# Reciprocal roots with a third-order last turn, and the key sum masked in one operation

## The reference

```
x = x + 0.5 * ffn(layernorm(x))
x = x + attention(layernorm(x))
x = x + 0.5 * ffn(layernorm(x))
```

```
q = elu(x @ Wq.T + bq) + 1;  k = elu(x @ Wk.T + bk) + 1;  v = x @ Wv.T + bv      # per head
kv = einsum('bthd,bthe->bhde', k, v)
denom = einsum('bthd,bhd->bth', q, k.sum(axis=1))
out = einsum('bthd,bhde->bthe', q, kv) / clip(denom, 1e-06)
return out @ Wo.T + bo
```

## Time and profile before

| | us |
|---|---|
| median of 3 runs | 501.38 |
| lowest, highest | 501.27, 502.42 |
| the profiled execution | 502.21 |
| its span, first to last instruction | 500.4 |

### The profile page before, as it was taken

The page is one execution under the profiler, slowest core; times in us unless marked ns, Lnnn a source line. Parts: engine busy times, 40 slices in busy tenths (PEclk is TensorE's granted clock), DMA queues, the critical chain, the costliest instruction groups (busy, mean ns, idle before and its releaser), DMA issues. The chain is left out here.

```text
span 500.4 us, 6022 instructions
## 1 busy us (share of the span) xinstructions
PE 345.3 (69%) x1710; PEld 281.1 (56%) x1710; DVE 351.1 (70%) x1084; ACT 235.6 (47%) x431; POOL 277.5 (55%) x302
## 2 busy tenths in 40 slices
PE   7913589999999353856769683400579999999500
PEld 6903367788888233545558562400558888888400
DVE  6798379988888445669888573720067888889674
ACT  3587156666676232444363441220056777766200
POOL 8000767666652475665557556657503777777730
PEclk9999999999999855899886687555699999999855
DMA  8920315656664411111111111111231232221399
GB/s 239 354 103 0 105 44 168 219 187 231 207 210 146 146 51 40 42 48 33 43 33 52 41 48 48 54 41 59 66 124 41 89 90 87 89 66 43 112 338 294
DMA packets 45216, 55.48 MB, mean 111 GB/s; under 512 B 6694, under 2 KB 28736, under 8 KB 45184
## 3 DMA queue, kind: packets, MB, share of 16 engines
q1 hardware_dynamic: 32304, 35.40, 21.2%
q0 software_dynamic: 8512, 17.60, 12.1%
q10 hardware_dynamic: 4368, 2.10, 1.4%
HBM read 25.98 MB, written 29.10 MB: 110 GB/s over the span
## 5 line engine op out<-in xcount | busy, mean ns | idle before, releaser
L1110 ACT ACTIVATE hf<-psum,bcol 128x512 f32<-128x512 f32 x128 | 88.4, 693 | 65.4 <-PE psum L1047 30.4
L1016 POOL DMA_INDIRECT xg<-xn_dram,gidx x64 | 67.2, 1050 | 69.3 <-POOLq L1683 38.5
L1002 POOL DMA_INDIRECT yt_dram<-y_sb,target x64 | 75.3, 1176 | 46.1 <-issue 23.2
L1147 DVE TENSOR_TENSOR hl<-hf,hh 128x512 fp32r<-128x512 f32 x128 | 87.2, 692 | 4.4 <-ACT hh L1112 1.4
L1262 POOL DMA_INDIRECT yg<-y_dram,slot x64 | 61.3, 958 | 48.8 <-issue 18.6
L833 POOL DMA_INDIRECT xs_dram<-xns,place x64 | 62.4, 976 | 33.3 <-issue 18.0
L1043 PE MATMUL psum<-xh,wres 128*128 128x512 f32 x128 | 53.7, 419 | 4.1 <-ACT xh L1095 2.7
L1136 DVE TENSOR_TENSOR xl<-psum,xh 128x512 fp32r<-128x512 f32 x32 | 21.9, 684 | 46.2 <-ACT xh L1095 46.2
L1058 PE MATMUL psum<-hh,wres 128*128 128x512 f32 x128 | 52.5, 410 | 0.0
L1047 PE MATMUL psum<-xl,wres 128*128 128x512 f32 x128 | 51.2, 400 | 0.8 <-DVE xl L1136 0.7
L1044 PE MATMUL psum<-xh,wres 128*128 128x512 f32 x128 | 50.9, 397 | 0.0
(11 more groups left out here) (239 smaller groups left out, 722.1 us busy)
## 6 DMA issues: line engine op xcount, KB each, us to landing
yt_dram<-zeros SPq DMA_DIRECT2D x24, 256.0 KB
ring<-yt_dram SPq DMA_DIRECT2D x24, 256.0 KB
xs_dram<-zeros SPq DMA_DIRECT2D x16, 288.0 KB
xg<-xs_dram SPq DMA_DIRECT2D x16, 288.0 KB
wexp_raw<-in_L_ffn_w SPq DMA_DIRECT2D x16, 256.0 KB, 6.0
y_dram<-y_rows_out SPq DMA_DIRECT2D x16, 256.0 KB
x_sb<-in_L_attn_x SPq DMA_DIRECT2D x8, 256.0 KB, 4.0
xn_dram<-xns SPq DMA_DIRECT2D x8, 256.0 KB, 6.6
```

Source lines behind the costliest of these rows:

```text
L1002: gp.indirect_dma_start(out=yt_dram, out_offset=bass.IndirectOffsetOnAxis(ap=target[:, j:j + 1], axis=0), in_=self.y_sb[:, s % YG, t], in_ ...
L1016: gp.indirect_dma_start(out=self.xg[:, s % 4, t], out_offset=None, in_=xn_dram, in_offset=bass.IndirectOffsetOnAxis(ap=gidx[:, j:j + 1], a ...
L1110: one = nc.scalar.activation(self.hf[:, c], bank[1 + c][:], ACT.Relu, bias=bcol[:, at:at + 1])
L1147: dve.tensor_tensor(self.hl[:, s % 2, c], self.hf[:, c], self.hh[:, s % 2, c].bitcast(F32), ALU.subtract).then_inc(hl_ready[c], 1)
```

## The change

The last two of the three Newton turns are replaced by one turn of third order, with four operations: a scaled square, the product with the variance, `(a + shift) * a`, and `(a + constant) * y`. So 3 x 3 operations become 3 + 4, in both versions; in the lists of steps there are two fewer places to yield. `vv` gets 16 columns of ones in place of one, so TensorE's key sum is 144 columns wide and the key sum stands in 16 columns already. `block_mask` gets the 16 columns of `head_mask` behind its 128, and one VectorE operation over 144 columns masks both. `kv_masked` counts one for each group.

```diff
+LAST_SQUARE, LAST_SHIFT = 1.2247449159622192, 2.041241407394409
+KEY_SQUARE, KEY_SHIFT = 19.595918655395508, -4.082482814788818
...
-        block_mask = sb("block_mask", [P, P])
+        block_mask = sb("block_mask", [P, C + HEADS])
...
-            for turn in range(3):
-                ch.add(dve.tensor_tensor(a, y, y, ALU.mult))
+            for turn in range(2):
+                if turn == 0:
+                    ch.add(dve.tensor_tensor(a, y, y, ALU.mult))
+                else:
+                    ch.add(dve.scalar_tensor_tensor(a, y, LAST_SQUARE, y, ALU.mult, ALU.mult))
                 done = ch.n
                 yield
                 ch.wait(done)
...
-                ch.add(dve.scalar_tensor_tensor(rstd[:, ts] if turn == 2 else y, a, 1.5, y, ALU.add, ALU.mult))
+                if turn == 1:
+                    ch.add(dve.scalar_tensor_tensor(a, a, LAST_SHIFT, a, ALU.add, ALU.mult))
+                    done = ch.n
+                    yield
+                    ch.wait(done)
+                ch.add(dve.scalar_tensor_tensor(rstd[:, ts] if turn == 1 else y, a, 1.875 if turn == 1 else 1.5, y, ALU.add, ALU.mult))
...
-                passed = {(0, 1): {2: (kv_masked, 2 * (NG - 2)), 4: (yg_used[0], NG), 6: (yg_used[1], NG)},
+                passed = {(0, 1): {2: (kv_masked, NG - 2), 4: (yg_used[0], NG), 6: (yg_used[1], NG)},
...
-                self.vv = new("vv", [P, 2, GT, C + 1])
+                self.vv = new("vv", [P, 2, GT, C + HEADS])
...
-                        last = nc.tensor.matmul(bank[4][:, 0:C + 1], self.kk[:, n % 2, t], self.vv[:, n % 2, t], start=(t == 0), stop=(t == GT - 1))
+                        last = nc.tensor.matmul(bank[4][:, 0:C + HEADS], self.kk[:, n % 2, t], self.vv[:, n % 2, t], start=(t == 0), stop=(t == GT - 1))
...
-                    pe.wait_ge(kv_masked, 2 * n + 2)
+                    pe.wait_ge(kv_masked, n + 1)
...
-                    for square in (64.0, 16.0, 4.0):
+                    for square in (64.0, KEY_SQUARE):
...
-                        to = self.rsa[:, u, 0] if square == 4.0 else y
-                        ch.add(dve.scalar_tensor_tensor(to, a, -3.0, y, ALU.add, ALU.mult))
+                        if square == KEY_SQUARE:
+                            ch.add(dve.scalar_tensor_tensor(a, a, KEY_SHIFT, a, ALU.add, ALU.mult))
+                            done = ch.n
+                            yield
+                            ch.wait(done)
+                            ch.add(dve.scalar_tensor_tensor(self.rsa[:, u, 0], a, 7.5, y, ALU.add, ALU.mult))
+                        else:
+                            ch.add(dve.scalar_tensor_tensor(y, a, -3.0, y, ALU.add, ALU.mult))
...
-                    dve.tensor_tensor(self.kv[:, u, 0:C], bank[4][:, 0:C], block_mask[:], ALU.mult).then_inc(kv_masked, 1)
-                    dve.tensor_tensor(self.kv[:, u, C:C + HEADS], head_mask[:], bank[4][:, C:C + 1].to_broadcast([P, HEADS]), ALU.mult).then_inc(kv_masked, 1)
+                    dve.tensor_tensor(self.kv[:, u], bank[4][:, 0:C + HEADS], block_mask[:], ALU.mult).then_inc(kv_masked, 1)
...
+                ch.add(nc.gpsimd.tensor_copy(block_mask[:, C:C + HEADS], head_mask[:]))
...
-                nc.gpsimd.memset(attention.vv[:, :, :, C:C + 1], 1.0).then_inc(ones_col, 1)
+                nc.gpsimd.memset(attention.vv[:, :, :, C:C + HEADS], 1.0).then_inc(ones_col, 1)
```

More of the change, by code:

```diff
@@ L1719, in _ @@
                 ch.then(nc.gpsimd.affine_select(out=head_mask[:], in_=head_mask[:], compare_op=ALU.is_ge, fill=0.0, base=HD - 1, pattern=[[HD, HEADS]], channel_multiplier=-1))
-                ch.add(nc.gpsimd.tensor_copy(block_mask[:].rearrange("p (h d) -> p h d", d=HD), head_mask[:].unsqueeze(2).to_broadcast([P, HEADS, HD])))
+                ch.add(nc.gpsimd.tensor_copy(block_mask[:, C:C + HEADS], head_mask[:]))
+                ch.add(nc.gpsimd.tensor_copy(block_mask[:, 0:C].rearrange("p (h d) -> p h d", d=HD), head_mask[:].unsqueeze(2).to_broadcast([P, HEADS, HD])))
                 ch.add(nc.gpsimd.iota(iota_lo[:], pattern=[[1, P]], base=0, channel_multiplier=0, **fl))
```

## The result

| | before | changed |
|---|---|---|
| median | 501.32 (496.55 to 502.42, 4 runs) | 505.50 (504.47 to 509.46, 4 runs) |
| ratio, 95% interval | | 1.0094 [1.0054, 1.0135] |
| profiled execution | 502.21, span 500.4 | 504.62, span 502.9 |

The kernel became 0.9% slower. A ratio in this document leaves out executions in the slower state that the core shows now and then, so it is not simply the quotient of the two medians. The forecast was 498.5 us, its range ended at 501.6, and slower had a chance of 0.10.

A forecast was written before the change was run, and what follows sets the result against it. Attention, a chain of latencies, was taken to set GpSimd's last start at 329.17 us. Half of 1.8 (rounds 1 and 3), 0.9, plus 0.82 + 1.03 + 0.05 + 0.1 gave 2.9 us: median 498.5 us, range 495.7 to 501.6.

The forecast's parts named there:

- What bounds the kernel, and from where on: Everything after GpSimd's last start at 329.17 us moves with that instant; from there to the end 171.2 us stay unchanged.
- Round 1, 1.4 us: Attention round 1: two slow scale steps fewer, 0.70 us each, bring the norm 1.4 us earlier; ends 0 and 1.4.
- half of 1.8 kept: Rounds 1 and 3 give 1.8 us; unexplained waits before 224.81 and 309.22 may eat it, so 0.9 counted.
- B: Rival: late completions before 309.22 do not move and swallow the gain; 0 to 1.5 us left, 500.6 us; chance 0.25.
- Rounds 4 and 5, 0.82 and 1.03: Attention: the last scale step comes where the third last was, 0.82 us earlier in round 4, 1.03 in round 5.
- Rounds 6 and 7, 0: Attention: scale comes earlier, but TensorE works without a gap (6) and a late TensorE completion holds ScalarE (7): 0.
- Round 3, 0.4: Attention round 3: two scale steps of 0.20 us fewer, 0.4 us, less than ScalarE's wait of 1.56.
- The routing scales, 0 and 0.1: Routing rows' scales: first stage's two calls 0, hidden by VectorE's wait for logits; last two calls 0.1 us together.
- the rule that was set against the rows: VectorE: each operation starts only after the pipe empties, so 28 removed operations of 0.16 us give some 4.5 us.
- The mask, net 0.05: One mask operation of 0.30 us for a pair of 0.36; less the wider key sum, 0.05 us for rounds 6 and 7.
- D: Rival: shifted work meets TensorE's low clock, 3.1 us per round; two rounds lost give 504.7 us; chance 0.12.

The follow-up runs named there:

- i1: Kernel before with attention's 56 fetches and 64 sends as plain transfers, rows not the tokens'; 463.70 us, ratio 0.9213 where the kernel before takes 502.92.
- i2: Changed kernel with attention's fetches and sends as plain transfers, rows not the tokens'; 460.37 us, ratio 0.9154 where the kernel before takes 502.92.
- g1: Changed kernel, but GpSimd fetches group 3 only when TensorE has projected k and v of group 1; 515.03 us, ratio 1.0226 to the kernel before.
- h1: Kernel before with attention's fetches and sends as plain transfers, rows not the tokens'; 461.74 us, ratio 0.9662 where the kernel before takes 477.82.
- h2: Changed kernel with attention's fetches and sends as plain transfers, rows not the tokens'; 456.49 us, ratio 0.9577 where the kernel before takes 477.82.
- h4: Changed kernel with attention's transfers plain and the old scale in round 1; 462.83 us, ratio 0.9646 where the kernel before takes 477.82.
- g2: Changed kernel, but round 1 of attention's scales keeps its three turns of three operations; 504.82 us, ratio 1.0011 to the kernel before.
- e4: Changed kernel with two empty steps ahead of each scale's last step, restoring the order of before; 478.64 us, ratio 0.9991 to the kernel before.
- f1: Kernel before, unchanged, run once for its trace on a chip where its median is 502.57 us; 507.22 us.
- f2: Changed kernel again, unchanged, where the kernel before takes 502.57 us; 507.27 us, ratio 1.0113.
- e2: Kernel before with both shorter Newton scales only, mask and key sum as before; 475.76 us, ratio 0.9933 where the kernel before takes 478.62.

## Why the prediction failed

- **What bounds the kernel, and from where on.** Right in the comparison that was forecast: the end followed GpSimd's last start by 171.1 us. It is no fixed length, though: between i1 and i2 it grew by 2.4.
- **Round 1, 1.4 us, and "half of 1.8 kept".** This is the step that failed, in sign. The term itself came (1.7 us for 1.4), and what lay behind it was wrong: "if these delays move with the work, gains pass; if they end at an instant of their own, all before them is lost". The prediction asked only how much of the gain the late waits would eat; B, its rival on them, ended at zero. They grew instead: rounds 1 to 3 took 29.07 us for 23.34. With round 1 as before the ratio is 1.0011, with it early 1.0113 (on another chip of the kind): the early norm costs about 5 us. How it does so is argued and not shown. The prediction named GpSimd's fetch of groups as what round 1 needs, and never asked what the norm of round 1 sets off: the next fetch, which in the kernel before came after 3.74 us of rest and in the changed one after 1.64. But g1 gave that fetch a longer rest and was slower still (1.0226), so a short rest alone does not explain the loss. Without lateness the term is 0.5 to 0.9 (from round 0 to 1 12.58 us in h1 and 12.12 in h2, 12.51 in i1 and 11.63 in i2; h4 against h2 0.8), between its two ends.
- **Rounds 4 and 5, 0.82 and 1.03.** The mechanism was right where completions come in time: chip 2 gives 0.9936 and all of it goes when the places in the order are filled up again. The sizes: round 5 gave 1.9 in i2, twice the term, round 4 half a microsecond (11.54 from round 3 to 4 in i1, 11.03 in i2). On the late chips g2, which keeps these rounds, shows no gain in its time; its trace has it up to round 6 and loses it from 6 to 7.
- **Rounds 6 and 7, 0.** Wrong, and smaller than round 1. Where completions come in time the changed kernel loses 0.7 us from round 6 to 7 (11.57 in i2, 10.85 in i1), in the first comparison 2.5. e4, with the order of before, has 10.77. The prediction had put both at nothing, because TensorE works without a gap (6) and a late completion holds ScalarE (7): it allowed for no gain, and not for a loss. No run takes this apart.
- **Round 3, 0.4.** From round 2 to 3, 10.93 in i1 and 11.01 in i2: nothing.
- **The routing scales, 0 and 0.1.** On chip 5 1.0026 [0.9992, 1.0060], no gain. That each of the 28 operations would give its 0.16 us (4.5), the rule that was set against the rows, is refuted by e4: all are gone and the ratio is 0.9991.
- **The mask, net 0.05.** Right: 0.31 us for 0.30 forecast, and 1.0009 [0.9976, 1.0041] with the wider key sum. It ran alone on chip 2 only.
- **D.** Its mark was there: the granted clock of 203 to 237 fell from 1.00 to 0.78, and a round cost 3.1 more of TensorE's time. As an explanation it fell short, since the 4.0 us lost first are idle at an equal clock, and g2's median has no loss although the clock of its trace over 203 to 237 is 0.85. That slower came, to which D had given 0.10, does not show its mechanism. Its part in the rest of the loss was not measured by itself.

What stays open: why completions come late on some chips and not on others, and whether the index itself or the longer issue of each transfer brings it. That the lateness follows long rows of such transfers is seen in five traces (the changed kernel, f1, f2, g1, g2) and was moved by one edit, but the length of a row was not varied by itself. Nor is it explained why every shortened scale makes the way from round 6 to 7 longer, and so much longer on late chips. No version beat both kernels on both kinds of chip: e2 is the fastest with the real transfers on chip 2, and was not run on the others. A version with GpSimd's rows broken up by several pauses was not tried.

## What to carry to other kernels

Before pricing an edit as "this comes earlier", list what the earlier event releases, on GpSimd and the DMA queues above all, and look at what those queues are in the middle of. A wait that costs nothing in the trace may still be what keeps two things from meeting. Where a trace has waits that no record explains, the sum made from it holds for that chip: a bound of zero on them isn't enough, and a rival in which they grow has to be priced.

## What the hardware showed that was not expected

- One kernel, two kinds of chip: 501 to 505 us on some, 478 on others. Of the 27.4 us between the changed kernel's two profiled executions (504.62 and 477.23), 25.5 lie in attention, where the slower one has waits that no record explains and the faster one none. Such waits stand in every late chip's trace with indexed transfers in attention (7.17 us for `qe` in the changed kernel), and in none of chips 2 and 14. Small dependent steps of VectorE start 0.70 us apart in some of them (the kernel before, f2) in place of 0.20. With plain transfers of as many packets a late chip takes 463.7 us, within 2 of the other kind.
- The level of TensorE's clock goes with more time than this change is worth: 4 us between runs of one kernel (h2: 455.8 to 456.6 at 0.887, 460.5 and 460.6 at 0.877).
